# First four heads' q and k by way of memory: 8 larger transfers in place of 24 direct moves on the chip

## What is computed

```python
x = x + ret(layernorm(x), ...)                 # retention, 4 heads
x = x + ffn(layernorm(x), W_r, W_k, W_v, ...)  # channel mix
# attention: 16 heads of 16 channels, over 1024 tokens
q, k, v = proj(wq, bq), proj(wk, bk), proj(wv, bv)
scores = einsum('bhqd,bhkd->bhqk', q, k) / sqrt(16)
attn = softmax(scores + bias)                  # bias by relative distance
x = x + einsum(attn, v) @ wo + bo
x = x + ffn(layernorm(x), W_r, W_k, W_v, ...)  # channel mix again
# ffn: sigmoid(xr @ W_r) * (relu(xk @ W_k) ** 2 @ W_v)
```

## Time and profile before

| | before |
|---|---|
| median of 3 runs | 3125.78 us (3123.59 to 3126.05) |
| the profiled execution | 3130.65 us |
| its span | 3128.9 us |
| PE busy | 2909.2 us, 93% of the span |
| DVE busy | 2050.5 us, 66% |
| ACT busy | 1734.6 us, 55% |
| POOL busy | 1252.8 us, 40% |
| bytes moved by DMA | 107.58 MB |

### The profile page before, as it was taken

How to read it: one execution, slowest core, us unless ns; L and a number is a source line. 1 busy time by engine, 2 the same in 40 slices (tenths; PEclk the granted TensorE clock), 3 DMA queues, 4 the chain that set the end, 5 groups by cost and what they waited for, 6 DMA issues and landing times.

```text
span 3128.9 us, 51535 instructions
## 1 busy us (share of the span) xinstructions
PE 2909.2 (93%) x18786; PEld 1509.1 (48%) x18786; DVE 2050.5 (66%) x4319; ACT 1734.6 (55%) x3667; POOL 1252.8 (40%) x1764
## 2 busy tenths in 40 slices
PE   5989999899998999989999999999999999998997
PEld 3643356433564336643466434653346533465334
DVE  4469735796357954589545894459934599346982
ACT  2428834388344873448634585336854368443784
POOL 2225533255232543335433354334543345333453
PEclk8979999899999999999999999999999999999998
DMA  6041000500005000140001400023000320003200
GB/s 174 1 106 17 2 1 3 123 25 2 1 11 124 15 2 1 23 113 16 1 1 42 94 15 1 1 55 81 16 1 1 81 55 15 1 1 81 55 2 14
DMA packets 54779, 107.58 MB, mean 34 GB/s; under 512 B 12400, under 2 KB 34976, under 8 KB 54400
## 3 DMA queue, kind: packets, MB, share of 16 engines
q1 hardware_dynamic: 54528, 104.29, 14.4%
HBM read 56.66 MB, written 36.72 MB: 30 GB/s over the span
## 4 chain that ended last, share of the span: by engine, by line
PE 70%; DVE 13%; issue 4%; SPq 4%; POOL 3%; ACT 3%; DMA 3%; POOLq 0%; ACTq 0%; DVEq 0%
PE psum L736 18%; PE psum L785 15%; PE psum L554 11%; DVE mx L1448 7%; PE psum L762 4%; PE psum L836 4%; SPq L446 3%; PE psum L817 2%; PE psum L885 2%; PE psum L871 2%; PE psum L589 2%; PE psum L625 2%; PE psum L888 2%; DMA parts<-mixed 2%; POOL X L1554 1%
## 5 line engine op out<-in xcount | busy, mean ns | idle before, releaser
L1448 DVE TENSOR_REDUCE mx<-psum 128x1 f32<-128x512 f32 x2048 | 1262.0, 684 | 126.4 <-PE psum L736 125.9
L1191 ACT ACTIVATE Z<-psum 128x512 f32<-128x512 f32 x2048 | 1120.6, 597 | 273.7 <-PE psum L762 241.9
L1644 POOL TENSOR_TENSOR Z<-Z,band_exp 128x256 f32<-128x256 f32 (+1 forms) x1152 | 713.1, 641 | 733.6 <-ACT Z L1191 727.1
L736 PE MATMUL psum<-SK,SQ 63*128 63x512 f32 x2048 | 805.4, 479 | 68.9 <-DVE mx L1448 44.1
L762 PE MATMUL psum<-SQ,SK 64*128 64x512 f32 x2048 | 788.9, 463 | 6.1 <-DMA SQ<-mrow 6.0
L785 PE MATMUL psum<-Z,Vx 128*17 128x256 f32 x8192 | 641.5, 388 | 0.1
L736 PEld LDWEIGHTS psum<-SK,SQ 63*128 63x128 f32 x2048 | 332.2, 193 | 527.0 <-DVE mx L1448 384.1
L554 PE MATMUL psum<-Wqkvg,Z 128*128 128x512 f32 x768 | 378.9, 618 | 19.0 <-ACT Z L1089 19.0
L762 PEld LDWEIGHTS psum<-SQ,SK 64*128 64x128 f32 x2048 | 323.8, 189 | 75.7 <-ACT Z L1191 55.8
L785 PEld LDWEIGHTS psum<-Z,Vx 128*17 128x17 f32 x8192 | 138.3, 95 | 354.4 <-issue 291.8
L1589 POOL TENSOR_TENSOR Z<-Z 128x512 f32<-128x512 f32 x64 | 81.2, 1269 | 353.9 <-DVE Z L1370 347.8
(11 more groups left out here) (121 smaller groups left out, 3275.2 us busy)
## 6 DMA issues: line engine op xcount, KB each, us to landing
parts<-Z SPq DMA_DIRECT2D x32, 512.0 KB
X<-L_attn_a_x SPq DMA_DIRECT2D x8, 1024.0 KB, 5.5
SQ<-parts SPq DMA_DIRECT2D x32, 256.0 KB, 7.6
SK<-parts SPq DMA_DIRECT2D x32, 256.0 KB, 10.8
SQ<-parts SPq DMA_DIRECT2D x16, 512.0 KB, 7.2
SK<-parts SPq DMA_DIRECT2D x16, 512.0 KB, 13.7
out<-X SPq DMA_DIRECT2D x16, 512.0 KB, 19.8
SQ<-mixed SPq DMA_DIRECT2D x96, 64.0 KB, 2.3
```

Source lines behind the costliest of these rows:

```text
L736: pe.matmul(row_bank(c), SQ[rows_of(h, MAX_ROW), h // 2, i * P:i * P + P], SK[rows_of(h, MAX_ROW), h // 2, 512 * k:512 * k + 512], start=T ...
L1191: nc.scalar.activation(ring[:, n % RING, :], col_bank(n), ACT.Exp)\
L1448: nc.vector.tensor_reduce(mx2[:, blk % 2, col, k:k + 1], row_bank(2 * u + k), AX_X, ALU.max)\
L1644: nc.gpsimd.tensor_tensor(ring[:, n % RING, a:z], ring[:, n % RING, a:z], band_exp[:, 4 * hg + COLS[i], at:at + z - a], ALU.mult)\
```

## The change

`spread_directly` and its semaphores go. `parts_store` of the first group stores all 8 heads (128 partitions) where it stored heads 4 to 7 (64 partitions), and `spread_rows` brings the first share from memory too, with 8 transfers, ahead of the second share. `spread[0]` takes the place of `spread_first`: the first score row waits for 8 transfers of it. The relu of the last mix, and the exponentials, keep their wait for the stores and lose the one for the direct moves.

```diff
-        spread_first = [tally("sp", f"spread_first_{side}", 12, 16) for side in "qk"]
-        spread = [None] + [tally("sp", f"spread{share}", 8, 16) for share in (1, 2)]
+        spread = [tally("sp", f"spread{share}", 8, 16) for share in range(3)]
...
-            def spread_directly(b, s):
-
-                need(sp, c_lo, b, 3 + s)
-                stack = (SQ_words, SK_words)[s]
-                for h in range(4):
-                    for group, part in enumerate(((1, 0, 0), (0, 1, 0))[s]):
-                        r0 = HALF * (h % 2) + HD * group
-                        sp.dma_start(stack[r0:r0 + HD, h // 2, :],
-                                     split[0][s][HD * h:HD * h + HD, part, :].bitcast(F32))\
-                            .then_inc(spread_first[s].sem, 16)
-
             def parts_store(b, h, s):
 
                 need(sp, c_lo, b, 4 * h + 3 + s)
-                p0 = (64, 0)[h]
                 done = (first_out, parts_out)[h][s]
                 for part in range(PARTS):
                     slot = (1 - part, part)[s]
-                    sp.dma_start(parts_scratch[s, (4, 8)[h]:8 * h + 8, slot],
-                                 split[h][s][p0:P, part, :].bitcast(F32)).then_inc(done.sem, 16)
+                    sp.dma_start(parts_scratch[s, 8 * h:8 * h + 8, slot],
+                                 split[h][s][:, part, :].bitcast(F32)).then_inc(done.sem, 16)
 
             def spread_rows(b, share, s):
 
                 heads = SHARES[share]
-                need(sp, (first_out, parts_out)[share - 1][s], b, 2)
+                need(sp, (first_out, parts_out)[share // 2][s], b, 2)
...
             for b in range(B):
 
-                for s in range(2):
-                    spread_directly(b, s)
                 for h in range(2):
                     for s in range(2):
                         parts_store(b, h, s)
                     if h == 0:
-                        for s in range(2):
-                            spread_rows(b, 1, s)
+                        for share in (0, 1):
+                            for s in range(2):
+                                spread_rows(b, share, s)
...
             def rows_wait(b, u):
 
-                if u == 0:
-                    need(pe, spread_first[0], b, 12)
-                    need(pe, spread_first[1], b, 12)
-                for share in (1, 2):
+                for share in range(3):
                     if u == NT * SHARES[share].start:
                         need(pe, spread[share], b, 8)
...
                 if q == 2:
-                    need(act, spread_first[0], min(b + 1, B - 1), 12)
                     need(act, first_out[0], min(b + 1, B - 1), 2)
...
                 for s in range(2):
-                    need(act, spread_first[s], b, 12)
                     need(act, first_out[s], b, 2)
```

## The result

The changed kernel takes **3185.41 us** (median of 4 runs, 3180.72 to 3198.24) beside 3125.91 for the kernel before (4 runs, 3123.59 to 3129.18): a ratio of 1.0196, 95% interval 1.0165 to 1.0227, 59.5 us or 1.9% slower. The forecast was 26.1 us slower, with a range up to 3175. The sign was right; the size is more than double and lies outside the range. The profiled execution took 3198.24 us, 12.8 above its median (that of before lay 4.7 above), so I read the places of the change in it and not its whole span.

The account below looks back on a forecast made before the run. Direct-move issue and ACT's wait for q's store were taken to bound each entry's start. Six entries at 4.2 us, 2.8 for entry 4, less 2.4, plus 0.5 for entry 0 made 26.1: 3125.78 to 3152 us, range 3137 to 3175.

Parts of the forecast that it names:

- What bounds the kernel: Each entry's start: first scores at +17.0 and ACT's relu free at +24.0 after c_lo(3); the relu decides.
- ACT's wait goes to nothing: ACT's relu before the last norm: q's store lands at +8.8, before ACT's own work ends at +13.8; 1.5 us returns.
- The round trip: Stores and spreads through memory ahead of the first score: it starts at +22.0 instead of +17.0, 5.0 us later (4.0 to 6.0).
- may cost 1 us: Upper bound on the first score's delay: k's full-size store holds twice the engines, and eight spreads queue right behind.
- The clock: PE after its longer idle: low clock adds 0.7 us to the 7.7 from first score to the norm's transposes.
- the slower rival: PE stays at the low clock in every entry as in entry 4: 45 us slower, 3171 us; 20% chance.
- the clock at 0.50 for 10 us in every entry: Sign in the profile, PE's granted clock, that would show the kernel slower than forecast.
- Entry 0: First score about 5.1 us late, but PE's 4.61 us idle before the maxima's transfer absorbs most: 0.5 us, at most 4.
- The late low stretches of entries 1, 3 and 6: Low clock behind PE's idle for ACT goes: could return 1.6 us each, half counted, 2.4 us in all.
- Faster: the new stores are not held to half of the engines: Round trip under 18.5 us gains: 3119 us at 373 GB/s, 3101 if PE never waited; together 5% chance.

Follow-up runs that it names:

- e1_alone: Changed kernel with one more wait: the spreads of heads 4 to 7 are issued only when those of heads 0 to 3 have landed; 3181.68 us.
- e4_store_first: Kernel before, direct moves kept, with q's two stores issued ahead of the 24 direct moves; 3158.18 us.
- e6_narrow: Changed kernel with each store of heads 0 to 7 cut into two of 4 heads, same bytes; 3236.91 us.
- e2_wide: Changed kernel with a head's parts interleaved in the memory tensor, so a store is 128 rows with one stride; 3097.54 us.
- e3_warm: Changed kernel with 22 dummy products on PE ahead of the first score in entries 1 to 7; 3226.01 us.
- e9_by_head: Kernel before with interleaved memory tensor, q's stores first, head 0's direct moves ahead of the others, and a wait for each head alone; 3085.43 us.
- e7_before_wide: Kernel before, direct moves kept, with the interleaved memory tensor alone; 3112.94 us.

## Why the prediction was right in direction and wrong in size

**What bounds the kernel: right.** The first score and the relu are what the change moves in entries 1 to 7.

**ACT's wait goes to nothing: right**, and q's store keeps its time though it carries twice the bytes: 9.6 us for 8.8 forecast, with the share at 0.51 as put.

**The round trip, the step that failed.** The term was +5.0 per entry with bounds of 4.0 to 6.0; it measured 25.5 - 17.0 = 8.5. The working took the sequence of heads 4 to 7 over from the trace and allowed "may cost 1 us" for k's store holding twice the engines. At entry 2 the 3.8 us beyond +22.0 split so: 0.8 more until q's store has landed, 0.7 more until k's has, and 2.3 more from the first k spread's issue to the last landing (10.0 instead of 7.7). Of the last, 0.9 is the queue behind, by e1_alone. The other 1.4 I put down to the pile-up, whose two halves e4_store_first and e6_narrow show: a store on few engines delays what comes behind it, and k's spreads are quick where q's had mostly landed. The events of the changed kernel show both at work there too, in each of entries 1 to 7: of the first q spread's 16 events, 8 come within 0.6 us, from 2.6 to 3.0 us after its issue on, and 12 in the kernel before, as many as k's store leaves free of the 16 (in e2_wide, whose store holds all alike, all 16 come together, after 4.0); and when the first k spread is issued fewer of q's 64 have landed, 21 at entry 2 where before it was 31. How much of the 1.4 us each half makes is not isolated. The prediction had named the mechanism and put at most 1 us on it, with no row. One place in the trace of before would have warned: at entry 0 the q spreads of heads 8 to 15 are issued at 220.95 beside k's full-size store, on 8 engines, and took (from issue to landing)

```profile
DMA to landing us min/median/max: 6.4/10.0/13.0
```

where those of heads 4 to 7 took 4.1 to 5.4 at entry 2. They carry twice the bytes, so this row gives no clean size for the delay either. Over seven entries the miss of the round trip is 3.5 x 7 = 25 us.

**The clock, under-sized.** Forecast: transposes 7.7 + 0.7 = 8.4 after the first score (entry 4: 10.6). Measured 9.43 on average, three entries at 10.5 or more: 1.0 x 7 = 7 us more. The 7.7 was no clean base either: e3_warm and e9_by_head show 6.0 where PE has not idled, so the kernel before, at entry 2, already paid 1.7 for its 2.1 us of idle. The sign that the prediction named for the slower rival, the clock at 0.50 for 10 us in every entry, came true: in entries 1 to 7 it is low for 13.6 to 17.1 us at a time, PE's idle included. The rival itself, transposes after 10.6 everywhere, was half right: they came so late in three of seven entries.

**Entry 0, a miss.** Forecast 0.5 and at most 4, measured 6.7. The first score is 8.1 late (25.0 after c_lo(3)), and the 4.6 of idle took only part of it: the first scores for the exponentials come 51.7 us after c_lo(3) instead of 48.8, and PE had idled 14.3 us ahead of the first score (timeline of PE; c_lo(3) at 177.84):

```profile
202.88 1.22 PE L719 MATMUL psum<-SK,SQ 63*128 63x512 f32 x3 [14.30 <-DMA SK<-parts]
...
229.50 0.76 PE L745 MATMUL psum<-SQ,SK 64*128 64x512 f32 x1
```

For the rest I have only the clock: it stays at 0.50 until about 240 us, where before it rose at about 231. I had not carried the clock to entry 0 in the forecast itself.

**The late low stretches of entries 1, 3 and 6: right in kind, twice the size.** From the transposes to the first maxima these took 31.7 us and the others 30.05; now all take 30.0. That returned 5.0 us, of which I had counted half.

**The sum** is 26.1 + 25 + 7 + 6 - 2.6 = 61.5 us beside the measured 59.5.

**The rivals.** "Faster: the new stores are not held to half of the engines" was right about what decides: with the layout of e2_wide that condition holds, the first score comes at 16.2 (under its 18.5) and the time is 3097.5, near its far end of 3101. It was wrong only about this kernel, whose shape holds the stores to half.

## What to carry to other kernels

Before making transfers fewer and larger, look at the leading size of both sides: here a store whose side in memory was 8 heads by 16 rows ran on half of the DMA engines and the same bytes as 128 rows on all, and this decided between 59.5 us lost and 29 won. A transfer on few engines costs twice, because transfers behind it that need all engines wait for those few, as the landing events of e6_narrow show. Where an engine waits for a batch of transfers, let it wait for what its first instruction reads and order the queue that way: PE's short idle is paid again in its clock afterwards.

## What the runs showed of the hardware that I had not expected

- Busy share and rate go with the leading size of the store: 4 heads 0.26 and 107 GB/s, 8 heads 0.51 and 205, 128 rows 1.01 and 406.
- Moves of 64 KB that follow a narrow store on the same queue issue at 0.89 us each instead of 0.63 and land after 5.1 us instead of 2.4; behind a wide store 0.68.
- The clock's price is not in step with the idle. No idle or one of up to 1.7 us: the transposes 6.0 after the first score (once 9.1, after 1.6); 2.0 to 2.9 us: 6.0 to 7.6 in e7_before_wide; 3.8: 7.6 to 10.5; 6.2: 7.8 to 10.6 in e4_store_first; 10 to 11: 8.3 to 10.6. Which of these an entry gets at the same idle stays open.
